# Kernel mixing of a graph layer: features of two heads formed side by side, KV and mix products taken in pairs

## What is computed

```python
def _L0_mix_ref(hidden_states, Wq, Wk, Wv, Wo, Wf):
    ...
    qf = jax.nn.elu(q @ Wf.T) + 1.0
    kf = jax.nn.elu(k @ Wf.T) + 1.0
    kv = jnp.einsum('bshf,bshd->bhfd', kf, v)
    out = jnp.einsum('bshf,bhfd->bshd', qf, kv)
    k_sum = kf.sum(axis=1)
    norm = jnp.einsum('bshf,bhf->bsh', qf, k_sum)[..., None] + 1e-06
    out = (out / norm).reshape(b, s, D)
    return out @ Wo.T
```

## Time and profile before

| What | Value |
| --- | --- |
| median of 3 runs | 1055.28 us (1054.25 to 1058.2) |
| the profiled execution's own time | 1058.6 us |
| its span, first to last instruction | 1056.8 us |
| PE busy | 1011.2 us, 96% |
| DVE, ACT, POOL busy | 784.4, 638.2, 143.6 us |
| mean granted TensorE clock | 0.99 of full speed |

### The profile page before, as it was taken

One profiled execution on the slowest core, in us unless ns is written; L12 is line 12 of the kernel. 1 busy time (PEld: TensorE's weight loads), 2 busy tenths in 40 slices (PEclk: granted clock), 3 DMA queues, 4 the chain that ended last, 5 costly groups with the idle time before them and its releaser, 6 DMA issues.

```text
span 1056.8 us, 15069 instructions
## 1 busy us (share of the span) xinstructions
PE 1011.2 (96%) x5227; PEld 868.8 (82%) x5227; DVE 784.4 (74%) x1078; ACT 638.2 (60%) x825; POOL 143.6 (14%) x185
## 2 busy tenths in 40 slices
PE   3999999999999999989999799999999999999998
PEld 3899999998797999978788777788888878788775
DVE  6337878774858768867774588888888879788687
ACT  3357766632321223589883467877777777777572
POOL 2002223231010101243220110000000000000013
PEclk9999999999999999999999899999999999999989
DMA  8652323336545675211104399999999999999996
GB/s 289 185 180 61 110 70 88 93 113 176 171 143 160 179 220 159 80 58 63 41 1 165 99 356 359 389 377 382 354 382 368 379 360 381 369 363 372 329 325 234
DMA packets 140508, 237.33 MB, mean 225 GB/s; under 512 B 6908, under 2 KB 48124, under 8 KB 137892
## 3 DMA queue, kind: packets, MB, share of 16 engines
q1 hardware_dynamic: 135780, 225.91, 62.8%
q0 software_dynamic: 1760, 6.37, 1.6%
q10 hardware_dynamic: 2912, 4.34, 1.1%
HBM read 206.56 MB, written 30.03 MB: 224 GB/s over the span
## 4 chain that ended last, share of the span: by engine, by line
PE 78%; DVE 7%; issue 4%; ACT 4%; DMA 3%; POOL 2%; SPq 1%; ACTq 0%; DVEq 0%; POOLq 0%
PE bank L1296 33%; PE bank L961 6%; PE bank L963 6%; PE bank L962 5%; PE bank L975 4%; PE bank L977 4%; PE bank L976 4%; PE bank L1178 2%; DMA raw<-in_wffn 2%; PE bank L1095 2%; DVE wlo L1370 1%; PE bank L1192 1%; PE bank L1283 1%; PE bank L1204 1%; PE bank L1037 1%
## 5 line engine op out<-in xcount | busy, mean ns | idle before, releaser
L1667 DVE TENSOR_TENSOR wlo<-raw,whi 128x2048 fp32r<-128x2048 f32 x72 | 164.6, 2288 | 27.6 <-ACT whi L859 27.3
L859 ACT ACTIVATE a_all<-raw 128x2048 fp32r<-128x2048 f32 x72 | 138.1, 1918 | 50.3 <-DMA raw<-in_wffn 23.3
L859 ACT ACTIVATE whi<-raw 128x2048 fp32r<-128x2048 f32 x72 | 137.9, 1916 | 41.7 <-DMA raw<-in_wffn 25.2
L1370 DVE TENSOR_TENSOR wlo<-raw,whi 128x1024 fp32r<-128x1024 f32 (+1 forms) x72 | 120.0, 1671 | 46.4 <-ACT whi L651 45.4
L651 ACT ACTIVATE whi<-raw 128x1024 fp32r<-128x1024 f32 (+1 forms) x72 | 89.0, 1241 | 96.1 <-PE bank L963 47.7
L1667 DVE TENSOR_TENSOR t_all<-raw,a_all 128x2048 fp32r<-128x2048 f32 x36 | 82.5, 2292 | 41.6 <-ACT a_all L859 41.2
L961 PE MATMUL bank<-a_all,whi 128*128 128x384 f32 x320 | 109.1, 341 | 0.0
L963 PE MATMUL bank<-a_all,wlo 128*128 128x384 f32 x320 | 107.5, 336 | 0.0
L1296 PE MATMUL bank<-a_all,xg 128*128 128x512 f32 x360 | 107.0, 411 | 0.4 <-DVE t_all L1667 0.4
L962 PE MATMUL bank<-a_all,whi 128*128 128x384 f32 x320 | 107.4, 336 | 0.0
L1296 PE MATMUL bank<-whi,t_all 128*128 128x512 f32 x288 | 100.4, 410 | 0.0
(11 more groups left out here) (276 smaller groups left out, 2092.3 us busy)
## 6 DMA issues: line engine op xcount, KB each, us to landing
raw<-in_wffn SPq DMA_DIRECT2D x144, 512.0 KB
raw<-in_wffn SPq DMA_DIRECT2D x72, 1024.0 KB
raw<-in_wall SPq DMA_DIRECT2D x28, 1024.0 KB
raw<-in_wall SPq DMA_DIRECT2D x32, 512.0 KB
yrows<-zero SPq DMA_DIRECT2D x24, 512.0 KB, 7.0
y_rows<-zero SPq DMA_DIRECT2D x8, 1024.0 KB, 8.6
dense<-yrows SPq DMA_DIRECT2D x8, 512.0 KB, 8.0
y_rows<-dense ACTq DMA_DIRECT2D x16, 256.0 KB, 5.8
```

The costliest lines, as they stand in the source:

```text
L859: act.activation(hi_ring[u % RAW], raw[:, u % RAW, :], ACT.Copy).then_inc(hi_done, 2)
L1370: dve.tensor_tensor(ring(wlo, k), part(k), ring(whi, k).bitcast(F32), ALU.subtract).then_inc(lo_done, width(k))
L1667: dve.tensor_tensor(lo_ring[u % RAW], raw[:, u % RAW, :], hi_ring[u % RAW].bitcast(F32), ALU.subtract)\
```

## The change

The work is regrouped over pairs of steps. An even step forms the k features of both heads of a pair, an odd step the q features of both. Within a group the matmuls alternate: one for the even head (partitions 0 to 63, one bank), one for the odd head (partitions 64 to 127, the next bank). The KV products of a pair open the next even step, ahead of the piece, in two parts of bank 0. The mix products of a pair open the odd step behind it, in banks 1 and 0. ACT, DVE and the semaphore counts follow.

```diff
         def feature(h, i):
 
+            g, part_ = i % 2, i // 2
             b = gp_bank("feat", 4 * h + i)
...
+            if h % 2:
+                return qf[g][:, part_, :], b[:, 0:N]
+            if part_ == 0:
+                return kf[g][:, 0:2, :], b[:, :].rearrange("p (t f) -> p t f", t=2)
+            return kf[g][:, 2, :], b[:, 0:FD]
...
-                act.wait_ge(feat_done, 4 * h + 2)
-                if h >= 2:
-                    act.wait_ge(mix_full, h - 1)
-                act.activation(qf_s[h % 2][:, 0, :, :], qf[h % 2], ACT.Copy).then_inc(qf_hi, 1)
+                if h % 2:
+                    act.wait_ge(feat_done, h + 1)
+                    if h >= 3:
+                        act.wait_ge(mix_full, h - 1)
+                    for g in range(2):
+                        act.activation(qf_s[g][:, 0, :, :], qf[g], ACT.Copy).then_inc(qf_hi, 1)
...
+                if h >= 2 and h % 2 == 0:
+                    kv_high(h - 2)
+                    kv_high(h - 1)
...
-                if 1 <= h <= H:
-                    kv_high(h - 1)
...
+                if h >= 2 and h % 2 == 0:
+                    pe.wait_ge(feat_done, h - 1)
+                    if h >= 4:
+                        pe.wait_ge(kv_ready, h - 2)
+                        pe.wait_ge(mix_done, h - 2)
+                    for g in (h - 2, h - 1):
                         for f in range(2):
+                            for t in range(NT):
+                                last = pe.matmul(kv_bank(g)[:, f * (HD + 1):(f + 1) * (HD + 1)], kf[g % 2][:, t, f * P:(f + 1) * P],
+                                                 v_tok[:, t, g, :], start=(t == 0), stop=(t == NT - 1))
+                        last.then_inc(kv_full, 1)
+                if h >= 3 and h % 2:
+                    mix(h - 3)
+                    mix(h - 2)
...
+                        rows_ = [slice(0, HD), slice(HD, P)]
+                        if h % 2:
+                            f = slice(i // 2 * P, i // 2 * P + P)
                             for n, (x_part, w_part) in enumerate(((0, 0), (0, 1), (1, 0))):
+                                for g in range(2):
+                                    last = pe.matmul(b[g][:, 0:N], wf_s[rows_[g], w_part, f], qk[h // 2 % 2][rows_[g], 0, x_part, :],
+                                                     start=(n == 0), stop=(n == 2))
+                                    if n == 2:
+                                        last.then_inc(gp_full, 1)
...
                 k = PAIRS + 2 + h
+                if h >= 3 and h % 2:
+                    mix_out(h - 3)
+                    mix_out(h - 2)
                 for n in ahead(k):
                     lo(n)
...
+                    dve.wait_ge(kv_hi, h)
```

More of the change, by code:

```diff
@@ L1026, in _, with mix @@
             pe.wait_ge(bo_added, 1)
+            def mix(g):
+                pe.wait_ge(kv_ready, g + 1)
+                if g >= 2:
+                    pe.wait_ge(mix_done, g - 1)
+                pe.wait_ge(qf_lo, g + 1)
+                for n, (kv_part, q_part) in enumerate(((0, 0), (0, 1), (1, 0))):
+                    for f in range(2):
+                        last = pe.matmul(bank[1 - g % 2][:, 0:N], kv[g % 2][:, kv_part, f, :], qf_s[g % 2][:, q_part, f, :],
+                                         start=(n == 0 and f == 0), stop=(n == 2 and f == 1))
+                last.then_inc(mix_full, 1)
             for h in range(H + 2):
                 k = PAIRS + 2 + h
[L1029 to L1035, removed]
-                        for f in range(2):
-                            last = pe.matmul(bank[1][:, 0:N], kv[g % 2][:, kv_part, f, :], qf_s[g % 2][:, q_part, f, :],
-                                             start=(n == 0 and f == 0), stop=(n == 2 and f == 1))
-                    last.then_inc(mix_full, 1)
+                if h >= 2 and h % 2 == 0:
+                    pe.wait_ge(feat_done, h - 1)
[3 more added lines that the diff above has]
+                    for g in (h - 2, h - 1):
+                        for f in range(2):
+                            for t in range(NT):
[5 more added lines that the diff above has]
+                    mix(h - 2)
                 if k < T_V:
@@ L1045, in _ @@
                     piece(k, ring_bank(k - T_V)[:, 0:N], A_hi, A_lo)
[L1046 to L1055, removed]
@@ L1450, in _, with mix_out @@
             qk_low(0, 1)
+            def mix_out(g):
+                own, other = (slice(HD * (p % 2), HD * (p % 2) + HD) for p in (g, g + 1))
+                o = bank[1 - g % 2]
+                dve.wait_ge(mix_full, g + 1)
+                if g >= 4:
+                    dve.wait_ge(mix_norm, (g - 4) // 2 + 1)
+                dve.tensor_scalar(norm[own, g // 2 % 2, :], o[other, 0:N], 1e-6, None, ALU.add).then_inc(norm_ready, 1)
+                dve.tensor_copy(moT[own, g // 2, :], o[own, 0:N]).then_inc(mix_done, 1)
             def invert(c, half):
@@ L1460, in _ @@
                 k = PAIRS + 2 + h
+                if h >= 3 and h % 2:
+                    mix_out(h - 3)
+                    mix_out(h - 2)
                 for n in ahead(k):
                     lo(n)
-                if h >= 2:
-                    g = h - 2
+                for g in (h - 2, h - 1) if h >= 2 and h % 2 == 0 else ():
                     own, other = (slice(HD * (p % 2), HD * (p % 2) + HD) for p in (g, g + 1))
[L1466 to L1478, removed]
+                    b = kv_bank(g).rearrange("p (f d) -> p f d", f=2)
+                    dve.wait_ge(kv_hi, h)
                     dve.tensor_tensor(kv[g % 2][:, 1, :, own], b[:, :, 0:HD], kv[g % 2][:, 0, :, own].bitcast(F32), ALU.subtract)
@@ L1481, in _ @@
                                       kv[g % 2][:, 0, :, other].bitcast(F32), ALU.subtract).then_inc(kv_ready, 1)
+                if k < T_V:
+                    qk_low(h // 2 + 1, h % 2)
+                if h == H + 1:
+                    for j in range(2):
+                        t_low(j, j, 4)
                 if h < H:
```

51 lines of the change are left out of this document (24 added, 27 removed).

## The result

| | before | after |
|---|---|---|
| median of six runs, us | 1057.08 (1054.25 to 1058.2) | 1042.47 (1041.84 to 1045.54) |
| span of the profiled execution, us | 1056.8 | 1043.8 |
| first feature to first edge product, us | 165.7 | 151.6 |
| a pair of steps, us | 18.04 | 16.53 |

The ratio is 0.9877, 95% interval [0.9858, 0.9895]: the change makes the kernel faster by 1.2%. The forecast was 1043.3.

A forecast was written before the change was run, and what follows sets the result against it. PE, busy all of each 9.02 us step, was taken to bound the loop. Terms: 16.9 (features) - 5.6 (mix waits) + 1.0 (old waits) - 0.3 (first and last steps) = 12.0, so 1055.28 - 12.0 = 1043.3 us; range 1040.0 to 1051.0.

The forecast's parts named there:

- full overlap of the features of two halves: PE's q and k features at half the pitch: 2.11 us gained a pair, 16.9 in eight; full or nearly full 0.50.
- The rival with loads in a row: PE features: streams overlap but weight loads come one after another; 8.0 us gained, 1047.3 us; chance 0.24.
- the one without overlap: PE features stay at 4.22 us a pair; 1.6 us gained from waits, 1053.7 us; chance 0.12.
- the one with a passage at each change of half: PE features: some 0.1 us more on each matmul, 240 changes, 24 us, so slower at 1077.7 us; chance 0.07.
- The other estimate: PE features at 1.53 times for two tiles: 2.75 us, 1.47 gained a pair, whole time nearly the same.
- The wait at the mix product: PE waits 0.8 us for DVE at each pair's first mix product, seven times: 5.6 us given back.
- the rival of a longer chain: ACT and DVE hand-overs before the mix take 0.5 us more each round: 8.3 us gained, 1047 us; chance 0.07.
- The second ends near 9.8, ... so never last: POOL's second low part, wanted 1.16 us after the first mix starts, would never be what PE waits for.
- The end of the loop: At the last mix product PE waits 2.05 us as before, clock 0.81 there; left alone on both sides.
- The first steps: First and last steps slower: first two have features without products, first chain meets a busier ACT; 0.3 us taken off.
- old waits: PE's earlier waits for the KV halves, except the last, go away: 1.0 us gained.

The follow-up runs named there:

- e8: e4 plus, on DVE, mix-product copies ahead of the reciprocal and, in the last step, the first two `t_low` ahead of `lo`: 1038.44 us, again 1038.37 us.
- e2: The changed kernel with both heads' feature products on rows 0 to 63, still in two banks: 1054.36 us, ratio 0.9973.
- e5: The changed kernel with POOL's low parts of q cut to half their columns, except for the first two heads: 1043.36 us in one execution.
- e4: The changed kernel with DVE's low KV halves moved ahead of its `lo` in even steps: 1040.49 us, ratio 0.9859.
- e7: The kernel before, with DVE's low KV halves of the last head moved ahead of the mix copies: 1057.53 us, ratio 0.9999.
- e1: The changed kernel with feature matmuls grouped by half, runs of three for q, six and three for k, instead of alternating: 1044.14 us, ratio 0.9878.
- e9: The changed kernel with all the even head's feature matmuls ahead of the odd head's, runs of six for q, nine for k: 1048.53 us, ratio 0.992.

## Why the prediction was right, and where it was off

**The place and the mechanism of the gain** were right: full overlap of the features of two halves. The q starts take 1.07 us by the pitch (1.05 predicted), k 1.10 (1.06). e8, where nothing waits, has pairs of 16.0 against the 15.93 of my sum, so 2.04 us a pair are gained on PE, 16.3 in eight, where I had 16.9. The rival with loads in a row (1.34 and 2.02, pair 17.2), the one without overlap (e2 shows what that would look like) and the one with a passage at each change of half are out. The floor of 0.108 us for a load was taken from one set of rows, and e2, on one set, has 0.120; the k features at 0.061 are under it. This agrees with the Trainium skill, TensorEngine Tiling (Array Packing), Key Properties: different tiles load and multiply in parallel. The other estimate, made from the 3.07 times for four tiles in the Trainium skill, TensorE: Matmul & The Clock Gate, Measured speedup vs the span model, doesn't hold here: two tiles give 2.0 times, not 1.53. That PE can also pass matmuls of the busy half was no part of the prediction. One slip in the sums changes nothing: 1.14 less 0.1 over nine is 0.116; the 0.118 that I used is what the eight distances from 109.96 to 110.90 give.

**The wait at the mix product** was sized at 0.8 us a pair, 5.6 in all. Measured are 16.53 - 16.0 = 0.53 a pair, 3.7 in seven, and in two parts. The first mix waits only some 0.2. Counted from the q start at 129.21, the chain agrees up to `lo`: last sum done 5.33 (predicted 5.3), `lo` started 7.98 (7.8). But `lo` took 1.30, not 1.87, and the low KV half was ready at 9.68, not 10.25. The row that I took the 1.87 from contained a wait. So the rival of a longer chain is out too: this one was 0.57 us shorter. The term of the sum that was too large is this wait, 5.6 us in place of 3.7. Two more rows of the kernel before, from the timelines of POOL and DVE elsewhere in the loop:

```profile
105.41 1.84 POOL L547 TENSOR_TENSOR t_all<-dense,t_all 128x768 fp32r<-128x768 f32 x1 [7.17 <-ACT t_all L741]
```
```profile
106.47 1.86 DVE L1370 TENSOR_TENSOR wlo<-raw,whi 128x1024 fp32r<-128x1024 f32 x1
```

`lo` ends at 108.33 (106.47 + 1.86), 1.08 after POOL's op (105.41 + 1.84 = 107.25); in after it ends at 138.49, 1.10 after POOL's first (135.55 + 1.84 = 137.39, with the duration of the row above); in e5 1.08 after POOL's second. With POOL idle it takes 1.22 (130.21 above). By these rows the two don't run at the same time.

**"The second ends near 9.8, ... so never last"** was wrong. POOL's second low part ended 10.99 after the q start and is the second part of the wait, some 0.33. It is the same collision seen from the other side: POOL's two ops take 4.65 while `lo` runs between them and 3.65 when it doesn't (e4). e5 and e4 take it away, each in its own way. I had listed a wait for POOL among what would prove me wrong, and it was there; it is small.

**The end of the loop** I left alone on both sides, and that was wrong in my disfavour. The wait fell from 2.02 to 1.33, and the clock didn't fall after it. In after, this wait is the same chain as in the pairs: the mix starts 9.72 behind the q start (205.05 and 195.33), not the 10.25 of my sum. In before it hung on something else as well, DVE's copies out of the mix product, which had waited 0.96 us for POOL's scaling. From the mix start to the tenth piece matmul before took 4.28 us (219.81 to 224.09) where 1.16 + 9 x 0.174 = 2.73 is what it takes at full clock: 1.55 us. That the shorter wait is the reason fits all twelve profiles (clock 1.00 behind that place after waits of up to 1.34 in ten of them, the 0.68 of e2 and the 1.33 of after included; 0.81 over the 9 us after 2.02 in before and 2.27 in e7), but no experiment changed the wait alone, so the cause is not shown.

**The first steps** cost 0.85, not 0.3: the first q group and its passage take 1.84 (78.78 to 80.62) where 1.24 would do, and the first pair's two mix waits are 0.25 longer than the 0.53 of a later pair.

Together: 16.3 + 1.0 (old waits) + 0.7 + 1.55 (end) - 3.7 - 0.85 (first steps) - 0.7 (0.3 for the second mix at the end, 0.4 for the wait for `t_low` behind it, 211.58 to 212.14 for a pitch of 0.175) = 14.3, measured 14.1; 0.2 us I can't place. My sum was 12.0, and by the medians of these runs the change gives 14.6. That 1043.3 lies only 0.8 from 1042.47 is luck: the median that I subtracted from was 1.8 below that of the six runs. The sum itself was too small, by 1.9 for the wait and 1.55 for the end of the loop, against 0.6 too much for the features and 0.55 too little taken off for the first steps.

## What to carry to other kernels

Two matmul streams on 64 rows each cost as much as one if they use different halves of the array and different banks, and a run of up to three in one half is as good as strict alternation. When a shorter PE makes the helpers due, look for the small operation that PE wants behind a large one that it doesn't, and move it ahead: three such moves on DVE (e8) were worth 5.3 us here. A duration read from a row where DVE and POOL both work on SBUF may hold a wait for the other; look for a row of the same operation with the other engine idle before using it in a chain.

## What the runs showed that I had not expected

TensorE starts a matmul of the idle half ahead of up to three of the busy half that stand before it in the program (e1: two start together at 142.94, though the second stands three places behind; e9: the second head's first starts with three of the first head's still to come, and the groups take 1.61 and 1.86 us where no reach would give 2.10 and 2.12). So what I wrote of the kernel, that the order in the code is the order on each engine, is not true of TensorE's two halves. Other lengths of a run than 3, 6 and 9 were not tried. The Trainium skill, TensorE: Matmul & The Clock Gate, section The mechanism, has matmuls start and end in program order, without reordering. These rows speak against that for the two halves of the array.

DVE's subtraction of 128x1024 took 1.22 us alone and 1.86 beside POOL's, and POOL's two took 3.65 or 4.65 us, by who held the other up. The Trainium skill, SBUF — State Buffer, section SBUF: two separate sides, describes a port pair for which the two engines exclude each other for a whole instruction, and the trace agrees (108.33 and 138.49, each 1.1 after the end of POOL's; 1.08 in e5).
